# Token lists of the two expert layers: experts' list behind the rows' list, layer 0's gates behind the position sums, five weight remainders on VectorE

## The reference

```python
h = concat(patch_embedding(x), txt)                        # (16, 165, 256)
h = h + scan_layer(layernorm(h)) @ W_out
# layer 0's experts: the best of 4 groups, both experts of that group
macro = sigmoid(xf @ macro_w); micro = sigmoid(einsum('td,gde->tge', xf, micro_w))
w = top1_normalized(macro)[:, :, None] * top2_normalized(micro)
h = h + einsum('te,tef,efd->td', w, silu(xf @ gate_w) * (xf @ up_w), down_w)
h = h + attention(layernorm(h))
# layer 1's experts: the best 2 of 4, gates from a softmax over the two logits
h = h + sum_k gate_k * expert_k(layernorm(h))              # 256 -> 1024 -> 256, gelu
```

## Time and profile before

| | |
|---|---|
| median of 3 executions | 790.91 us (790.46 to 791.1) |
| the profiled execution | 791.43 us, span of its instructions 789.6 us |
| PE busy | 719.4 us, 91% of the span |
| DVE busy | 468.2 us, 59% |
| ACT busy | 375.5 us, 48% |
| POOL busy | 356.6 us, 45% |
| granted TensorE clock, mean | 0.966 |
| chain that ended last | PE 67%, DVE 15%, POOL 8%, DMA 3%, ACT 3%, issue 2% |

### The profile page before, as it was taken

The page is one execution under the profiler, slowest core; times in us unless marked ns, Lnnn a source line. Parts: engine busy times, 40 slices in busy tenths (PEclk is TensorE's granted clock), DMA queues, the critical chain, the costliest instruction groups (busy, mean ns, idle before and its releaser), DMA issues.

```text
span 789.6 us, 19052 instructions
## 1 busy us (share of the span) xinstructions
PE 719.4 (91%) x6285; PEld 632.7 (80%) x6286; DVE 468.2 (59%) x1241; ACT 375.5 (48%) x887; POOL 356.6 (45%) x310
## 2 busy tenths in 40 slices
PE   5989983899999999998798997989999999999991
PEld 4768973888888898778688986868888888888871
DVE  4998678444444444337888888945455454554540
ACT  5797657343333343334465665533444434434430
POOL 2539980322233223211676871043665555655331
PEclk9999995999999999999999999999999999999996
DMA  9970044114122111117121334411322233222225
GB/s 270 411 306 2 1 148 148 49 28 117 28 32 41 33 22 29 22 21 226 57 81 54 85 97 159 145 52 38 55 44 47 43 54 54 46 48 41 40 35 150
DMA packets 37192, 66.25 MB, mean 84 GB/s; under 512 B 3776, under 2 KB 29360, under 8 KB 35568
## 3 DMA queue, kind: packets, MB, share of 16 engines
q1 hardware_dynamic: 23696, 46.90, 17.7%
q0 software_dynamic: 13248, 18.21, 14.4%
q10 hardware_dynamic: 192, 0.38, 0.1%
HBM read 44.83 MB, written 23.35 MB: 86 GB/s over the span
## 4 chain that ended last, share of the span: by engine, by line
PE 67%; DVE 15%; POOL 8%; DMA 3%; ACT 3%; issue 2%; POOLq 0%; SPq 0%; DVEq 0%; ACTq 0%
PE PS L839 17%; PE PS L1046 15%; PE PS L1059 15%; PE PS L852 8%; POOL X L2050 6%; PE PS L1419 3%; PE PS L1446 1%; PE PS L1031 1%; DMA Y<-in_wtok_dram 1%; PE PS L1427 1%; POOL X L1671 1%; POOL X L2045 1%; PE PS L821 1%; DVE stats L2467 1%; DVE rs L2400 1%
## 5 line engine op out<-in xcount | busy, mean ns | idle before, releaser
L839 PE MATMUL PS<-Y,X 128*128 128x256 f16 (+1 forms) x1344 | 139.0, 258 | 1.6 <-issue 0.9
L839 PEld LDWEIGHTS PS<-Y,X 128*128 x1344 | 119.4, 98 | 18.2 <-issue 3.1
L1225 POOL DMA_INDIRECT sum<-X,dest x45 | 88.8, 1973 | 96.6 <-ACT X L1128 81.4
L1059 PE MATMUL PS<-X 128*128 x720 | 125.7, 273 | 2.0 <-ACT X L1128 1.9
L1046 PE MATMUL PS<-X 128*128 128x256 f16 (+1 forms) x768 | 122.6, 265 | 0.4 <-issue 0.4
L1118 ACT ACTIVATE X<-PS,X 128x256 f32<-128x256 f32 (+1 forms) x192 | 72.6, 461 | 103.3 <-PE PS L1046 100.2
L1046 PE MATMUL PS<-X,Y 128*128 128x256 f16 (+1 forms) x384 | 100.2, 264 | 0.0
L1059 PE MATMUL PS<-Y,X 128*128 x360 | 98.2, 273 | 0.0
L1017 POOL DMA_INDIRECT sum<-Y,dest x24 | 38.7, 1611 | 116.1 <-DVE Y L969 112.8
L1046 PEld LDWEIGHTS PS<-X 128*128 x768 | 71.8, 97 | 10.3 <-issue 0.9
L1059 PEld LDWEIGHTS PS<-X 128*128 128x128 f16 x720 | 70.4, 98 | 11.1 <-issue 3.1
(11 more groups left out here) (402 smaller groups left out, 1389.6 us busy)
## 6 DMA issues: line engine op xcount, KB each, us to landing
X<-in_w_dram SPq DMA_DIRECT2D x11, 1024.0 KB, 16.1
stage<-in_w_dram SPq DMA_DIRECT2D x16, 512.0 KB, 3.5
sum<-h SPq DMA_DIRECT2D x2, 2048.0 KB, 7.5
xs<-Y SPq DMA_DIRECT2D x2, 1040.0 KB, 5.4
xs<-Y SPq DMA_DIRECT2D x2, 1032.0 KB, 5.1
h<-in_txt_dram SPq DMA_DIRECT2D x2, 1024.0 KB, 17.3
Y<-in_patches_dram SPq DMA_DIRECT2D x3, 672.0 KB, 8.2
sum<-h SPq DMA_DIRECT2D x2, 768.0 KB, 6.4
```

The lines of the kernel that those rows point to most:

```text
L839: ins = nc.tensor.matmul(PS[:, 2 * u + half, c * T1:c * T1 + tokens], w_[:, at_:at_ + P], x_[:, slot, k, 0:tokens], start=(n == 0), stop=( ...
L1059: ins = nc.tensor.matmul(PS[:, 4 + a, 0:D], h_[:, s, c, a * P:(a + 1) * P], part[:, off:off + D], start=(s == 0 and c == 0 and n == 0), st ...
L1225: nc.gpsimd.indirect_dma_start(out=sum1, out_offset=bass.IndirectOffsetOnAxis(ap=dest[:, i:i + 1], axis=0), in_=y1buf[:, u % 2, i - first_ ...
```

## The change

Three edits. In `positions` the block that makes `source` and `dest` now stands ahead of the one that makes `slote`. Layer 0's gates become a function `row_gates` that `positions` calls once `posf` is there; `full` moves from `ra` to the unused `oh[:, 1]`, since `ra` still holds the logits that the sigmoid reads. And the low halves of chunks 14, 18, 21, 22 and 23 are made by DVE, in the loop ahead of pairs 5 and 7 and behind the last pair; POOL leaves them out and waits for `w0_split` behind each.

```diff
+DVE_LOW = {5: (14,), 7: (18,), NT // 2: (21, 22, 23)}
+BY_DVE = tuple(n for chunks_ in DVE_LOW.values() for n in chunks_)
...
-            full = raf[:, 0:4 * NFULL].rearrange("p (g k) -> p g k", g=4)
+            full = (raf if done else oh[:, 1].rearrange("p g t -> p (g t)"))[:, 0:4 * NFULL].rearrange("p (g k) -> p g k", g=4)
...
                 sum_over(chain, posf[:, c, :], total)
+            if meanwhile:
+                meanwhile()
...
+            dve.wait_ge(map_psum, done + 1)
+            tile_, row_, taken = (PS[:, 7, i * tiles:(i + 1) * tiles] for i in range(3))
+            from_, to = (tok[:, i, 0:tiles] for i in (1, 2))
+            chain.link(nc.vector.tensor_copy(from_, row_))
+            nc.vector.scalar_tensor_tensor(out=source[:, 0:tiles], in0=tile_, scalar=float(P), in1=from_, op0=ALU.mult,
+                                           op1=ALU.add).then_inc(source_ready, 1)
...
+            dve.sem_inc(dest_ready, 1)
             sf, sg_ = tok[:, 0, 0:tiles], tok[:, 1, 0:singles]
...
             nc.vector.tensor_copy(slote[:, 0:tiles], sf).then_inc(slots_ready, 1)
-            dve.wait_ge(map_psum, done + 1)
...
+            def row_gates():
+                dve.wait_ge(sig_ready, 1)
...
+                dve.sem_inc(pay_ready, 1)
+
+            positions(dve, chain, 1, SLOT0, 0, inrow0, intile0, PAIRS0, SINGLES0, row_gates)
...
             for n in range(EARLY, XW // CW):
+                if n in BY_DVE:
+                    continue
+                if n - 1 in BY_DVE:
+                    pool.wait_ge(w0_split, n)
                 split(n, 4 if n < SCANNED else 1)
...
+            def low_halves(at_):
+                for n in DVE_LOW.get(at_, ()):
+                    dve.wait_ge(w0_split, n)
+                    dve.wait_ge(w_high, n - BY_ACT[0] + 1)
+                    nc.vector.tensor_tensor(w0_low(n), w0_landing(n), w0_high(n), ALU.subtract).then_inc(w0_split, 1)
+
             for i in range(NT // 2):
+                low_halves(i)
                 dve.wait_ge(o_psum, i + 1)
...
+            low_halves(NT // 2)
             dve_rest(dve, chain, scales, newton)
```

More of the change, by code:

```diff
@@ L666, in dest_of_token, with positions @@
             chain.link(nc.vector.tensor_tensor(to, to, from_, ALU.add))
-        def positions(dve, chain, choices, tiles, done, inrow, intile, pairs, singles):
+        def positions(dve, chain, choices, tiles, done, inrow, intile, pairs, singles, meanwhile=None):
             hot = rc[:, 0:4, :]
@@ L731, in positions @@
                                         along(k_iota, P)[:, c0:c1], ALU.is_equal).then_inc(hot_ready, 1)
+            dve.wait_ge(map_psum, done + 1)
[4 more added lines that the diff above has]
+                                           op1=ALU.add).then_inc(source_ready, 1)
+            dve.wait_ge(source_ready, done + 1)
+            chain.link(nc.vector.scalar_tensor_tensor(out=from_, in0=tile_, scalar=float(P), in1=from_, op0=ALU.mult,
+                                                      op1=ALU.add))
+            dest_of_token(dve, chain, tiles, from_, to, taken)
+            chain.link(nc.vector.tensor_copy(dest[:, 0:tiles], to))
+            dve.sem_inc(dest_ready, 1)
             sf, sg_ = tok[:, 0, 0:tiles], tok[:, 1, 0:singles]
@@ L1319, in dve_rest @@
             first_max(chain, rc[:, 0:4, :], top, oh[:, 0], oh[:, 1], rc[:, 4:8, :])
[L1320 to L1336, removed]
@@ L1337, in dve_rest @@
-            dve.sem_inc(pay_ready, 1)
-            positions(dve, chain, 1, SLOT0, 0, inrow0, intile0, PAIRS0, SINGLES0)
+            def row_gates():
+                dve.wait_ge(sig_ready, 1)
+                chain.link(nc.vector.tensor_reduce(score, rb[:, 0:4, :].rearrange("p g t -> p t g"), AX, ALU.max))
+                chain.link(nc.vector.tensor_scalar(a, score, 1e-9, None, ALU.add))
+                chain.link(nc.vector.reciprocal(a, a))
+                chain.link(nc.vector.tensor_tensor(score, score, a, ALU.mult))
+                u = ra[:, 0:2, :]
+                micro = rb[:, 4:12, :].rearrange("p (g e) t -> p e g t", e=E0)
+                for e in range(E0):
+                    chain.link(nc.vector.tensor_tensor(rc[:, 0:4, :], micro[:, e], oh[:, 0], ALU.mult))
+                    sum_over(chain, u[:, e, :], rc[:, 0:4, :])
+                chain.link(nc.vector.tensor_tensor(a, u[:, 0, :], u[:, 1, :], ALU.add))
+                chain.link(nc.vector.tensor_scalar(a, a, 1e-9, None, ALU.add))
+                chain.link(nc.vector.reciprocal(a, a))
+                chain.link(nc.vector.tensor_tensor(a, a, score, ALU.mult))
+                for e in range(E0):
+                    chain.link(nc.vector.tensor_tensor(pay[:, :, D + e], u[:, e, :], a, ALU.mult))
+                dve.sem_inc(pay_ready, 1)
```

## The result

The changed kernel takes 793.2 us (median of 20 executions, 791.7 to 800.8), the kernel before 791.1 (20 executions, 789.0 to 792.5). The ratio is 1.0034 [1.0022, 1.0045]: slower, by 2.1 us as the medians give it and 2.7 as the ratio does. The profiled execution of the changed kernel took 795.33 us with a span of 793.5, 3.9 above the profiled span of before, so it lies at the slow end of its kernel, and the difference of the two profiled executions is larger than that of the medians.

What follows compares the result with a forecast made beforehand. In layer 0 the start of PE's unbroken stretch, set by `source` and the gathers, bounds the kernel; +0.15 + 2.3 - 1.1 + 1.7 = +3.05 against the profiled 791.43 gives 794.0 for the median, stated as 793.9, range 791.2 to 795.4.

Steps and rivals of the forecast that it cites:

- rival 1: The stores decide, but PE's clock falls in layer 0 only: +1.65 us, 792.6; chance 0.22.
- The low halves, +0.15: End of the loop: five low halves on DVE, the 4.00 us instruction shrinking to 0.2; +0.15 us, bounds -0.1 and +0.5.
- the 0.5 us named as a sign of being wrong: The prediction is wrong if the loop's end moves by more than 0.5 us.
- Rival 4: The 4.00 us instruction behind the loop isn't POOL's doing, so three low halves come on top: +3.8, 797.7; chance 0.05.
- `pay_ready` 5.4 us later: Layer 0: gates made after the counting's sums, so their signal comes at 130.4 instead of 124.95, 5.4 us later.
- Last landing 10.7 us behind it, POOL 0.85 us behind that: Layer 0: the last store lands 10.7 us behind `pay_ready`, at 141.15; POOL's first gather starts 0.85 us later, at 142.0.
- +2.3 was forecast: Layer 0: the first gather goes at 142.0 instead of 139.72, +2.3 us; bounds +1.75 and +2.8.
- Rival 3: Layer 0's stores land 8.7 us from the signal and don't decide: +0.3 there, no clock fall, 790.3; chance 0.08.
- The clock, +1.7: Layer 0: PE idles 3.4 us before the transposes, its clock falls, slowing transposes and products: +1.7 us.
- Rival 2: PE's clock holds in layer 0: +1.35, 792.3, or 790.9 if it holds in layer 1 too; chance 0.20.
- Layer 1's lists, -1.1: Layer 1: `source` made ahead of `slote` starts gathers and transposes earlier: -1.1 us, within -1.2 to -0.75.
- The order of the lists: Layer 0: `source` is ready 2.2 us earlier, but this buys nothing because POOL's wait for the stores ends at 141.15.

Runs made afterwards that it cites:

- three halves only: The whole change, but only chunks 21, 22 and 23 have their low halves on DVE, 14 and 18 stay on POOL: 793.35 us, ratio 1.0004.
- the second experiment: The kernel before with only the move of layer 0's gates, lists and low halves as before: 793.21 us, ratio 1.0034.
- 85 fillers: The whole change with 85 filler products instead of 30 ahead of layer 0's transposes: 791.9 us, ratio 1.0005.
- split store: The whole change, but the rows' 256 columns are stored without waiting for the gates, and the two gate columns separately behind `pay_ready`: 789.57 us, ratio 0.9976.

## Why the prediction was right

The forecast was 793.9, slower, in 791.2 to 795.4; measured were 793.2 and slower. By the number alone that decides little: 793.2 lies as near to rival 1 (792.6) as to the forecast (793.9). It is the traces that tell them apart. The cause is the one that the forecast named: `pay_ready` late, the stores behind it, the first gather behind those. Putting the gates back ahead of the counting takes all of the loss in layer 0 away, and moving the gates alone brings it back. Point by point:

**The low halves, +0.15.** Right. L2411 takes 0.18 us with POOL idle since 107.5 where it took 4.00, and the three halves behind the loop take 3.7 us in its place. In the trace's time the roots end 0.76 us earlier than before, but this execution was 0.87 ahead by PE's twelve 128x222 products, which stand in front of the loop. Before and changed:

```profile
53.95 2.79 PE L2302 MATMUL PS<-Y,wsm 128*96 128x222 f32 x12
```

```profile
53.08 2.80 PE L2313 MATMUL PS<-Y,wsm 128*96 128x222 f32 x12
```

Counted from the start of these products, the roots end 62.08 us later before and 62.06 and 62.07 in the two other kernels with the old loop; in the seven kernels of the table with all five halves on DVE it is 62.18 to 62.23. So the term is +0.13 on average. With three halves only it is 61.94: the two inside the loop cost about 0.25, and the three behind it bring about 0.1. By this count the end of the loop (58.0 us behind the products' start, 57.8 before) moved by less than the 0.5 us named as a sign of being wrong. Rival 4 is out. The Trainium skill, SBUF — State Buffer, section "Who interferes with whom", has a DVE `tensor_scalar` that uses both ports and a GpSimd instruction shut each other out for a whole instruction. The runs fit on both sides: 3.99 us again in the second experiment with POOL busy, 0.18 us without.

**`pay_ready` 5.4 us later.** Right to 0.1: 14.35 us behind the roots' end (129.62 - 115.27) against 8.90.

**Last landing 10.7 us behind it, POOL 0.85 us behind that.** Both sizes were wrong, in opposite directions, and that they nearly cancel is luck. Issued together, the three stores need 12.1 us from `pay_ready` in the profiled execution (11.0, 11.2 and 11.6 with the gates alone, 85 fillers and three halves), and POOL starts 0.29 us behind the landing. The 10.7 us had been read where the stores were issued one by one. The first gather, counted from the roots, moved by +3.1 there, +1.9 with the gates alone, +2.5 with three halves and +2.1 with 85 fillers: +2.4 on average, +2.3 was forecast. Rival 3 is out with its figure of 8.7 us: the engines were full, as this window of the changed kernel says (columns as in rows 5; the last two are the DMA share and GB/s), at no more than the 331 GB/s of the earlier trace rows.

```profile
132.00:139.50 7.50, 5.99 (x89) 5.82 (x86) 6.04 (x21) 1.40 (x3) 0.00 (x0) 0.78 1.07 317
```

**The clock, +1.7.** The fall came (4.09 us of pause where 3.4 was worked out, behind another of 2.08 where 1.5 was), and the transposes take the 1.11 us of the earlier trace rows. Its price is no constant. The first products took 2.2 us more in the profiled execution, 1.8 with the gates alone and 0.7 with three halves, by how soon after the transposes the clock was back. 1.7 is near their mean, 1.6. So the 1.7 fits the mean of three executions and none of them by itself, which is in part luck. More fillers gave back 1.3 by the medians, with about 1.1 spent on their own length. Rival 2 is out, and rival 1 too, since it wanted layer 1 at full clock: the transposes there took 1.11 us again (in the kernels with 85 fillers, with the split store and with three halves they took 0.65 or 0.66, but the first expert product came no sooner).

**Layer 1's lists, -1.1.** Nearly right: from the last list products to the transposes it takes 6.30 us (514.69 to 520.99), 7.45 before, which is -1.15; to the first expert product -0.92, since the half clock covers more of the products in between. The 0.8 us that the prediction allowed for PE's load of the expert number didn't come: the transposes start 0.2 us behind the end of the scale product. The seven kernels with the new order and layer 1 otherwise as it was lie at 10.96 to 11.14, the two with the old one at 11.96 and 11.98.

**The sum.** The profiled span moved by 3.9: -0.87 ahead of the loop (how this execution began), +0.11 from there to the roots' end, +3.04 to the transposes, +2.23 in the first products, -0.09 up to layer 1, -0.92 there, and 0.4 behind it that I can't place. The transposes, the first products and layer 1 make +4.4, where the forecast's terms for them make 2.9 (2.3 + 1.7 - 1.1); the kernel with three halves gives +2.4 by the same stages. The medians moved by 2.1, 0.9 less than the 3.0 forecast. What I had taken as two numbers are two spreads, of 1.2 and 1.5 us, and the forecast is near the middle of them. What a single execution has of each isn't settled by anything I found.

**One thing that it left out.** The order of the lists was booked as free of effect in layer 0 because the stores decided. With the stores out of the way it would still not have been seen: the fillers sized for the old order end last. With 12 instead of 30 they come 1.1 us earlier, 0.75 of it by the fillers.

## What to carry to other kernels

When two results are wanted by different engines, order them by what each still has to travel: the gates were cheap to compute, but 11 to 12 us of stores hung behind their semaphore. The chain that ended last named the last store and ACT's rows, not the gates: a late signal can hold back the transfers ahead of the one that the chain shows, so look too at where the DMA engines stand idle. Look for the place where the engine waits anyway (here the count on PE): there the early result costs nothing. A pause of TensorE ahead of a chain can be paid twice, by its length and by the clock behind it (4.09 us was, 1.43 us was not), so put filler products where it stands still, as many as the wait is long, and fewer where it is the last to arrive.

## What the runs showed of the hardware

- A 128x22 `tensor_scalar` on DVE stood for 4.00 us (3.99 in the second experiment) while POOL ran two instructions of 2.11 back to back; it didn't get in between them. With POOL idle it took 0.18. In one execution a 128x1536 addition on DVE stood for 12.23 us beside POOL's run of low halves, where it takes 1.85 and 1.96 in two others with POOL busy as well.
- POOL's indirect gather starts 0.29 us behind a DMA's landing and 0.90 us behind a DVE instruction's end (138.82 to 139.72).
- A store of 22 KB in 2816 pieces of 8 bytes took 8.1 us to land, against 4.8 to 5.3 for stores of about 1 MB issued as their rows came ready. A big store was under way beside it at first; in 135 to 136 us the DMA share was 1.27 at 8 GB/s.
- PE's clock can fall behind a pause of about 2 us and can also survive it: behind 2.16 us ahead of the scale product and then 12 fillers the transposes ran at half rate; with the split store, 2.07 us there, 30 fillers and 1.43 us more, they ran at full rate. With 85 fillers it fell to 0.50 behind the pause of 2.08 us, and in the whole change, the same program up to there, it stayed at 1.00. Which earlier pauses count, these runs don't separate.
